# Cross-attention in a decoder layer: one more key tile turned by DMA, fewer PSUM banks for TensorE's turns, two output banks

## The chip, the cores and the metric

The kernel runs on one core of a Trainium2 chip. The metric is device time in microseconds (us) of one execution; a lower time is better.

## The reference

One decoder layer with three parts, each followed by a residual sum and a layer norm. The change touches only the middle one, the cross-attention of 4 x 256 queries to 4 x 1601 keys, with 32 query heads that share 8 key heads of width 128. Cut to what matters:

```python
q = rmsnorm((x @ Wq.T) by heads, q_norm_w)            # 32 heads of 128
k = rmsnorm((ctx @ Wk.T) by heads, k_norm_w)          # 8 heads, each for 4 query heads
v = (ctx @ Wv.T) by heads
scores = einsum('bhqd,bhkd->bhqk', q, k) / sqrt(128) + mask
probs = softmax(scores, axis=-1)
out = einsum('bhqk,bhkd->bhqd', probs, v) @ Wo.T
```

Everything is float32; the kernel reaches that accuracy with two float16 parts of each operand, a high and a low one, and three products of them (high by high, low by high, high by low).

## The kernel before

The attention goes over 32 items (a batch entry and a key head) and cuts each into two units of 512 query rows, 64 units in all. A unit has four query tiles of 128 rows and 13 key tiles of 128 keys (the last holds 65). For each query tile TensorE makes the scores of all 1601 keys in four PSUM banks (`score`, nine matmuls of 416 columns and three of 354: three products in each bank), VectorE takes the mask off and finds the row's extreme (`subtract_mask`), and ScalarE makes the exponentials (`exp`). The probabilities then lie with queries on partitions, and the product with the values needs keys on partitions, so each key tile must be turned.

There are two ways of turning. **By TensorE** (`transpose_p`): four float32 transposes of 128 x 128 into one PSUM bank, then ScalarE casts the bank to the high part (`split_p` in `scalar`) and VectorE subtracts it for the low part (`split_p` in `vector`). The banks for this go round (`t_bank`, `TB` of them), and a turn waits until the low part of `TB` turns ago is made. **By DMA** (`turn_halves`): for each query tile j, an engine first casts the columns of the DMA's key tiles to float16 in `halves` and another subtracts for the low part; GpSimd and VectorE do it for j = 0 and 2, ScalarE and GpSimd for j = 1 and 3. Then the sync engine (SP) issues two transposing DMAs from `halves` into `pT_dma`, one for the high part and one for the low, eight in a unit. Their width is `DW = ND * P`, where `ND` is the number of key tiles that the DMA turns: 7 of 13.

A unit is written as 13 positions, one for each key tile's product with the values (`weigh_values`). Each engine's order is written out by hand: `P_AT` says at which positions the product takes a tile turned by TensorE, `D_AT` where it takes one of the DMA's, `TURN_AT` at which position TensorE turns which tile, `AT` at which positions the scores of the next unit's query tiles are made. All of the product goes into one bank (`o_bank`); VectorE's `take_o` scales it into `o_sb`, and the next unit's product waits for that at position 0.

SP issues every DMA of the attention from one queue, in order: per unit eight transposes (line 2192), four small stores of the inverse sums (line 2199), one load that spreads them to all partitions (`load_inverse`, line 2204, which first waits until those stores have landed), two stores of the output (line 2210), and in every second unit the next keys, queries and their roots (lines 2140 to 2148), in the others the next values (line 2157, and five small ones in line 2163). Each of its waits holds all that stands behind it in the queue. Four units make a trip; the first and the last of 16 trips are written out, and the others are a loop.

Next values are scaled by GpSimd at position 1 of every even unit (`scale_v`, line 2269) and split into their high halves by ScalarE at positions 3 and 6 (`split_v_hi`).

Of the kernel before, what the change touches and what calls it, by code (L numbers as in the profile page):

```python
# [24 lines left out]
P = 128  # L25
# [1917 lines left out]
def attention(chip, mask, qS, kS, vS, rS, iS, oS, output):  # L1943
# [15 lines left out]
    KR = KV - TAIL  # L1959
    HALF = P // 2  # L1960
    assert KR == HALF + 1
    TB = 3
    RING = 4
    BODY = 4
    TRIPS = UNITS // BODY
    ND = 7
    NP = NT - ND
    DW = ND * P
    P_AT = (0, 1, 2, 5, 8, 11)
    P_TILES = (7, 8, 9, 12, 10, 11)  # L1970
    TAIL_AT = P_TILES.index(NT - 1)
    D_AT = [pos for pos in range(NT) if pos not in P_AT]
    AT = {0: 1, 3: 2, 6: 3, 9: 0}
    TURN_AT = {2: 3, 5: 4, 8: 5, 10: 0, 11: 1, 12: 2}
    assert NP * BODY % RING == 0 and NP * BODY % TB == 0 and KP == NT * P and len(P_AT) == NP

    ends = [0, KP, KP + NT * HD, KP + NT * HD + 2 * QW]
# [18 lines left out]
    halves = [chip.at(f"halves{s}", [P, 2 * DW], 44160 + DW * s, F16) for s in range(2)]  # L1996
    pT_dma = [chip.at(f"pT_dma{s}", [P, 2 * ND, QW], place, F16) for s, place in enumerate((46976, 16768))]
    o_sb = chip.at("o_sb", [P, 2, QW], 51456)
    inv_b = chip.at("inv_b", [P, QW], 50560)
    t_min = chip.small("t_min", [P, 2 * QT])  # L2000
    p_sum = chip.small("p_sum", [P, 2 * QT])
    p_inv = chip.small("p_inv", [P, 32])
# [37 lines left out]

    def o_bank(i, u):

        return psum[:, SB - 1 if last_unit(i, u) else SB + TB, :]

    def banked(ap):
        return ap.rearrange("p (b n) -> p b n", b=SB)
# [14 lines left out]
    def last_trip(i):  # L2061
        return isinstance(i, int) and i == TRIPS - 1
# [3 lines left out]

    def last_unit(i, u):
        return last_trip(i) and u == BODY - 1

    def exists(i, u):  # L2070
        return u < BODY or not last_trip(i)
# [63 lines left out]
    def splits_v(i, u):  # L2135
        return not u % 2 and not (last_trip(i) and u)
# [217 lines left out]
    def gpsimd(pool):  # L2354
        def position(i, u, pos):
            after = exists(i, u + 1)
            if pos == 0 and after and not (first_trip(i) and u == 0):
                halves_hi_pool(pool, i, u + 1, 0)
                repeat_tail(pool, i, u + 1, 0)
            if pos == 1 and (splits_kq(i, u) or splits_v(i, u)):  # L2360
                pool.wait_ge(lo_dve, done_down(half_tile(i, u + 1, 0)))
            if pos == 1 and splits_kq(i, u):
                scale(pool, kq_item(i, u)[0])
                split_kq_lo(pool, *kq_item(i, u), 0)
            if pos == 1 and splits_v(i, u):
                scale_v(pool, v_item(i, u)[0])
            if pos == 3 and after:
                halves_lo_pool(pool, i, u + 1, 1)
                repeat_tail(pool, i, u + 1, 1)
            if pos == 5 and after:  # L2370
                halves_hi_pool(pool, i, u + 1, 2)
                repeat_tail(pool, i, u + 1, 2)
            if pos == 6 and splits_kq(i, u):
                split_kq_lo(pool, *kq_item(i, u), 2)
                split_kq_lo(pool, *kq_item(i, u), 1)
            if pos == 6 and splits_v(i, u):
                split_body_lo(pool, *v_item(i, u), 0)
                split_body_lo(pool, *v_item(i, u), 1)
            if pos == 9 and after:
                halves_lo_pool(pool, i, u + 1, 3)  # L2380
                repeat_tail(pool, i, u + 1, 3)
            if pos == 11 and splits_v(i, u):
                split_tail(pool, *v_item(i, u))
            if pos == 11 and first_trip(i):
                rows.root(pool, G // 2 - 1, 1, range(u, u + 1))
            if last_trip(i) and u >= BODY - 3:
                output.early["gpsimd"](pool, u - BODY, pos)

        halves_hi_pool(pool, 0, 1, 0)
        repeat_tail(pool, 0, 1, 0)  # L2390
        for n in range(2):
            split_kq_lo(pool, 1, 1, n)
        schedule(pool, position)
# [44 lines left out]
    def scalar(act):  # L2438
        def split_p(i, u, n):
            m, step = NP * u + n, turn_step(i, u, n)  # L2440
            act.wait_ge(pT_done, done(step))
            act.wait_ge(pv_done, done(pv_before(i, u, n)))
            act.copy(pT_hi[:, m % RING], t_bank(m)).then_inc(pT_hi_act, 1)  # L2443
            if n == TAIL_AT:
                for k, (to, at) in enumerate(((slice(96, 128), slice(32, 64)), (slice(96, 97), slice(64, 65)))):
                    act.wait_ge(pT_hi_act, done(scalar_step(i, u, n) + k))
                    act.copy(pT_lo[to, m % RING], pT_hi[at, m % RING]).then_inc(pT_hi_act, 1)

        def position(i, u, pos):
            after = exists(i, u + 1)  # L2450
            if pos in TURN_AT and exists(i, turn(u, pos)[0]):
                split_p(i, *turn(u, pos))
            if pos in (2, 5, 8) and after:
                exp(act, i, u + 1, TURN_AT[pos] - 2)
            if pos == NT - 1 and exists(i, u + 2):
                exp(act, i, u + 2, 0)
            if pos in (2, 8) and after:
                halves_hi_act(act, i, u + 1, TURN_AT[pos] - 2)
            if pos == 0 and splits_kq(i, u):
                split_kq_hi(act, *kq_item(i, u), 0)  # L2460
                split_kq_hi(act, *kq_item(i, u), 1)
            if pos == 3 and splits_kq(i, u):
                split_kq_hi(act, *kq_item(i, u), 2)
            if pos == 3 and splits_v(i, u):
                split_v_hi(act, *v_item(i, u), 0)
            if pos == 6 and splits_v(i, u):
                split_v_hi(act, *v_item(i, u), 1)
            if last_unit(i, u) and pos == 5:
                for s in range(2):
                    act.wait_ge(turned[s], turn_landed(2 * UNITS - 1))  # L2470
            if last_trip(i) and u >= BODY - 3:
                output.early["scalar"](act, u - BODY, pos)

        for n in range(3):
            split_p(0, 0, n)
        schedule(act, position)
# [100 lines left out]
    def tensor(pe):  # L2577
        def transpose_p(i, u, n):
            m, step, kt = NP * u + n, turn_step(i, u, n), P_TILES[n]
            if n == 0:  # L2580
                pe.wait_ge(e_done, done(tile(i, u, QT - 1)))
            if n == TAIL_AT:
                pe.wait_ge(tail_done, done(tile(i, u, QT - 1)))
            pe.wait_ge(pT_lo_done, done(step - TB))
            for j in range(QT):
                last = pe.transpose(t_bank(m)[:, P * j:P * (j + 1)], p_sb[u % 2][:, j, P * kt:P * (kt + 1)], ident)  # L2586
            last.then_inc(pT_done, 1)

        def weigh_values(i, u, pos):
            slot, kt = u // 2 % 2, tile_of(pos)  # L2590
            d = slice(HD * kt, HD * (kt + 1))
            if pos == 0:
                pe.wait_ge(v_lo_done, done(V_PARTS * (2 * i + u // 2 + 1) - 1))
                if not last_unit(i, u):
                    pe.wait_ge(o_done, done(unit(i, u) - 1))
            if pos == D_AT[0]:
                for s in range(2):
                    pe.wait_ge(turned[s], turn_landed(half_tile(i, u, QT - 1)))
            if kt < ND:
                product(pe, o_bank(i, u), v_hi[slot][:, d], v_lo[slot][:, d], pT_dma[u % 2][:, kt],  # L2600
                        pT_dma[u % 2][:, ND + kt], False, pos == NT - 1).then_inc(pv_done, 1)
                return
            n = P_AT.index(pos)
            m = NP * u + n
            pe.wait_ge(pT_lo_done, done(turn_step(i, u, n)))
            if kt < NT - 1:
                product(pe, o_bank(i, u), v_hi[slot][:, d], v_lo[slot][:, d], pT_hi[:, m % RING], pT_lo[:, m % RING],
                        pos == 0, False).then_inc(pv_done, 1)
                return
            pe.matmul(o_bank(i, u), v_hi[slot][:, d], pT_hi[:, m % RING], start=False, stop=False)  # L2610
            pe.wait_ge(pT_hi_act, done(scalar_step(i, u, n) + 2))
            pe.matmul(o_bank(i, u), v_lo[slot][:, d], pT_lo[:, m % RING], start=False, stop=False).then_inc(pv_done, 1)

        def position(i, u, pos):
            if pos in AT and exists(i, scored(u, pos)[0]):
                score(pe, i, *scored(u, pos))
            weigh_values(i, u, pos)
            if pos in TURN_AT and exists(i, turn(u, pos)[0]):
                transpose_p(i, *turn(u, pos))

        for n in range(3):

            pe.wait_ge(sem("qT_sb_done"), done(TT * G - 1 - 3 + n))
            transpose_p(0, 0, n)
        pe.wait_ge(sem("qT_sb_done"), done(TT * G - 1))
        pe.wait_ge(rows.summed, rows.summed_at(G - 1))
        schedule(pe, position)
# [471 lines left out]
```

## Time and profile before

| | |
|---|---|
| time, median of 3 runs | 2429.32 us (2429.22 to 2430.34) |
| time of the profiled execution | 2432.23 us |
| span from its first to its last instruction | 2430.4 us |
| TensorE (PE) busy | 2383.0 us, 98% |
| VectorE (DVE), ScalarE (ACT), GpSimd (POOL) busy | 75%, 66%, 60% |
| granted TensorE clock, mean | 0.998 of the higher level |
| transposing DMAs | 512, from 951.9 to 2213.3 us of the span |

The span begins with the gated projection and the keys and values, the attention's units begin near 976 us, and the output projection ends the span. Busy time of TensorE is modelled from pipelined matmuls whose times overlap, so a high share doesn't say by itself that TensorE is the limit. SP's issuing of DMAs isn't counted as busy time of an engine on the page; in the trace it appears as SPq, and SPq times are those of the sequencer that issues.

### The profile page before, as it was taken

How to read it: one execution, taken by the hardware profiler on the slowest of the kernel's cores; microseconds unless marked ns; L12 is line 12 of the kernel's file. 1: busy time of each engine (PE TensorE's matmuls, PEld its weight loads, DVE VectorE, ACT ScalarE, POOL GpSimd, SP SyncE). 2: the span in 40 equal slices, each digit the busy share in tenths (PEclk: the TensorE clock that was granted, in tenths of full speed). 3: DMA queues.
4: the chain of work that ended last, by engine and by line, in shares of the span. 5: the costliest groups of instructions: out<-in, count | busy, mean ns of one | idle time of the engine just before them, and what ended most of it. 6: DMA issues, size and time to landing. Idle time of an engine off the chain costs nothing.

```text
span 2430.4 us, 45071 instructions
## 1 busy us (share of the span) xinstructions
PE 2383.0 (98%) x12414; PEld 1650.8 (68%) x12414; DVE 1829.1 (75%) x2707; ACT 1593.3 (66%) x3248; POOL 1463.5 (60%) x1365
## 2 busy tenths in 40 slices
PE   9999999999999999999999999999999999999998
PEld 8878888888888886555555555555555555556887
DVE  5899999996865446777777777777777777776544
ACT  3187787787552556677777777777777777776321
POOL 0077877787640236787777777777777777763000
PEclk9999999999999999999999999999999999999999
DMA  6334433443364446888888888888888888879432
GB/s 232 119 101 120 130 106 110 130 112 112 120 211 135 150 133 199 196 177 194 186 197 182 196 183 202 193 184 197 185 198 183 198 183 200 193 145 244 149 109 65
DMA packets 749053, 398.43 MB, mean 164 GB/s; under 512 B 493265, under 2 KB 696145, under 8 KB 748977
## 3 DMA queue, kind: packets, MB, share of 16 engines
q1 hardware_dynamic: 748976, 397.52, 64.6%
q8 instruction: 35, 0.57, 0.1%
q14 instruction: 42, 0.34, 0.0%
HBM read 183.85 MB, written 96.11 MB: 115 GB/s over the span
## 4 chain that ended last, share of the span: by engine, by line
PE 45%; SPq 33%; issue 10%; DMA 8%; DVE 1%; POOL 1%; ACT 1%; POOLq 0%; ACTq 0%; DVEq 0%
SPq L2192 20%; PE banks L206 12%; PE banks L208 11%; PE banks L207 11%; PE banks L1137 8%; DMA inverse_sums<-p_invT 6%; SPq L2199 3%; SPq L2163 2%; SPq L2210 2%; PE banks L436 2%; SPq L2204 1%; SPq L103 1%; SPq L2140 1%; SPq L2157 1%; SPq L104 1%
## 5 line engine op out<-in xcount | busy, mean ns | idle before, releaser
L1058 DVE TENSOR_SCALAR_CACHE_REDUCE flags<-abs_s,thr 128x1376 bf16<-128x1376 f32 x256 | 403.7, 1643 | 1.1
L2521 DVE TENSOR_TENSOR pT_lo<-banks,pT_hi 128x512 f16<-128x512 f32 (+1 forms) x384 | 257.5, 684 | 157.2 <-ACT pT_hi L2443 157.2
L206 PE MATMUL banks<-k_hi,q_hi 128*128 128x416 f16 (+1 forms) x1024 | 342.9, 335 | 8.9 <-DVE t_min L2482 4.5
L207 PE MATMUL banks<-k_lo,q_hi 128*128 128x416 f16 (+1 forms) x1024 | 341.3, 333 | 0.0
L208 PE MATMUL banks<-k_hi,q_lo 128*128 128x416 f16 (+1 forms) x1024 | 341.1, 333 | 0.0
L2443 ACT CAST pT_hi<-banks 128x512 f16<-128x512 f32 x384 | 215.4, 585 | 161.9 <-PE banks L2586 160.9
L2482 DVE CUSTOM_DVE_ANT_0 p_even<-banks,minus_mask,guard_scalars 128x1664 f32<-128x1664 f32 x128 | 249.2, 1947 | 33.3 <-PE banks L208 33.2
L2482 DVE CUSTOM_DVE_ANT_0 p_odd<-banks,minus_mask,guard_scalars 128x1664 f32<-128x1664 f32 x128 | 249.4, 1948 | 30.3 <-PE banks L208 29.4
L2414 ACT ACTIVATE p_even<-p_even,t_min 128x1601 f32<-128x1601 f32 x128 | 209.3, 1635 | 3.0 <-DVE t_min L2486 2.2
L2414 ACT ACTIVATE p_odd<-p_odd,t_min 128x1601 f32<-128x1601 f32 x128 | 209.2, 1634 | 1.0 <-DVE t_min L2486 0.2
L914 ACT ACTIVATE k_sb<-banks,rstd 128x128 f32<-128x128 f32 x392 | 106.8, 384 | 114.6 <-POOL rstd L810 114.6
L206 PE MATMUL banks<-pT_dma,v_hi 128*128 128x512 f16 x448 | 169.8, 379 | 2.0 <-DMA pT_dma<-halves 2.0
L208 PE MATMUL banks<-pT_dma,v_lo 128*128 128x512 f16 x448 | 169.8, 379 | 0.0
L207 PE MATMUL banks<-pT_dma,v_hi 128*128 128x512 f16 x448 | 169.8, 379 | 0.0
L206 PEld LDWEIGHTS banks<-k_hi,q_hi 128*128 128x128 f16 x1024 | 99.9, 98 | 101.9 <-DVE t_min L2482 31.9
L2309 POOL TENSOR_TENSOR halves<-p_odd,halves 128x896 f16<-128x896 f32 x64 | 120.8, 1888 | 75.5 <-ACT halves L2300 75.5
L206 PE MATMUL banks<-kw_hi,c_hi 128*128 128x512 f32 x400 | 160.4, 401 | 0.6 <-DVE p_sb L350 0.4
L207 PE MATMUL banks<-kw_lo,c_hi 128*128 128x512 f32 x400 | 156.4, 391 | 0.0
L208 PE MATMUL banks<-kw_hi,c_lo 128*128 128x512 f32 x400 | 156.4, 391 | 0.0
L208 PEld LDWEIGHTS banks<-k_hi,q_lo 128*128 128x128 f16 x1024 | 100.4, 98 | 73.7 <-issue 0.4
L207 PEld LDWEIGHTS banks<-k_lo,q_hi 128*128 128x128 f16 x1024 | 100.5, 98 | 61.0 <-issue 0.6
L206 PE MATMUL banks<-pT_hi,v_hi 128*128 128x512 f16 x320 | 121.6, 380 | 18.5 <-DVE o_sb L2536 9.6
(286 smaller groups left out, 6512.3 us busy)
## 6 DMA issues: line engine op xcount, KB each, us to landing
raw<-keys SPq DMA_DIRECT2D x32, 800.5 KB, 4.5
keys<-kT_sb SPq DMA_DIRECT2D x50, 512.0 KB, 5.0
values<-v_sb SPq DMA_DIRECT2D x50, 512.0 KB, 3.6
raw<-values SPq DMA_DIRECT2D x32, 768.0 KB
queries<-qT_sb SPq DMA_DIRECT2D x64, 256.0 KB, 2.7
raw<-queries SPq DMA_DIRECT2D x32, 512.0 KB, 5.3
r_sb<-query_roots SPq DMA_DIRECT2D x32, 512.0 KB, 6.5
inv_b<-inverse_sums SPq DMA_DIRECT2D x64, 256.0 KB, 3.5
```

What stands on the lines that cost most here:

```text
L206: pe.matmul(out, a_hi, b_hi, start=start, stop=False)
L207: pe.matmul(out, a_hi, b_lo, start=False, stop=False)
L208: return pe.matmul(out, a_lo, b_hi, start=False, stop=stop)
L914: last = act.activation(k_sb[:, at], k_banks(s)[:, at], ACT.Copy, scale=rstd[:, s % RING, g:g + 1])
L1058: bits.done(dve.tensor_scalar(flags[:, tt % 2], abs_s[:, tt], thr[:, tt:tt + 1].bitcast(F32), 0.0, ALU.is_lt, ALU.add, accum_out=out[:, tt ...
L1137: last = pe.matmul(out, a[:, k], b, start=start and k + n == 0, stop=k == 1 and n == 2, skip_group_check=not start)
L2192: sp.dma_start_transpose(pT_dma[u % 2][:, ND * part:ND * (part + 1), P * j:P * (j + 1)], halves[j % 2][:, DW * part:DW * (part + 1)]).then ...
L2309: pool.tensor_tensor(halves[1][:, DW:2 * DW], p_sb[u % 2][:, j, 0:DW], halves[1][:, 0:DW], ALU.subtract).then_inc(lo_pool, 1)
L2414: act.activation(at, at, ACT.Exp, bias=t_min[:, n:n + 1], scale=-1.0, accum_out=p_sum[:, n:n + 1]).then_inc(e_done, 1)
L2443: act.copy(pT_hi[:, m % RING], t_bank(m)).then_inc(pT_hi_act, 1)
L2482: dve.tensor_tensor_reduce(banked(p_sb[u % 2][:, j, 0:KP]), psum[:, 0:SB, 0:SW], banked(minus_mask[:, j % 2]), guards.score_scale, 3.40282 ...
L2521: dve.tensor_tensor(pT_lo[r, m % RING], t_bank(m)[r], pT_hi[r, m % RING], ALU.subtract).then_inc(pT_lo_done, 1)
```

## The change

`ND` goes from 7 to 8: the DMA turns key tiles 0 to 7, TensorE tiles 8 to 12, five in place of six. `halves` and `pT_dma` grow with it, and `inv_b` moves to another place. `TB` goes from 3 to 2, and the bank that comes free becomes a second one for the output, so that units take them by turns; the product of a unit waits at position 0 for the output of the unit before the last one, not of the last one. TensorE's turn for the fourth tile stays at position 2, the fifth goes from position 5 to 6, and the sixth is gone. In the first unit alone, GpSimd scales the next values at position 5 and not 1, and ScalarE splits their first half at position 6 and not 3. `EXP_AT` writes out the same order of exponentials as before.

```diff
-    TB = 3
+    TB = 2
...
-    ND = 7
+    ND = 8
...
-    P_AT = (0, 1, 2, 5, 8, 11)
-    P_TILES = (7, 8, 9, 12, 10, 11)
+    P_AT = (0, 1, 2, 5, 9)
+    P_TILES = (8, 9, 10, 12, 11)
...
-    TURN_AT = {2: 3, 5: 4, 8: 5, 10: 0, 11: 1, 12: 2}
+    TURN_AT = {2: 3, 6: 4, 10: 0, 11: 1, 12: 2}
+    EXP_AT = {2: 1, 5: 2, 8: 3}
...
-    inv_b = chip.at("inv_b", [P, QW], 50560)
+    inv_b = chip.at("inv_b", [P, QW], 20864)
...
-        return psum[:, SB - 1 if last_unit(i, u) else SB + TB, :]
+        return psum[:, SB - 1 if last_unit(i, u) else SB + TB + u % 2, :]
...
+    def first_unit(i, u):
+        return first_trip(i) and u == 0
...
-            if pos == 1 and splits_v(i, u):
+            if pos == 1 and splits_v(i, u) and not first_unit(i, u):
                 scale_v(pool, v_item(i, u)[0])
...
+            if pos == 5 and first_unit(i, u):
+                scale_v(pool, v_item(i, u)[0])
...
-            if pos in (2, 5, 8) and after:
-                exp(act, i, u + 1, TURN_AT[pos] - 2)
+            if pos in EXP_AT and after:
+                exp(act, i, u + 1, EXP_AT[pos])
...
-                halves_hi_act(act, i, u + 1, TURN_AT[pos] - 2)
+                halves_hi_act(act, i, u + 1, EXP_AT[pos])
...
-            if pos == 3 and splits_v(i, u):
+            if pos == (6 if first_unit(i, u) else 3) and splits_v(i, u):
                 split_v_hi(act, *v_item(i, u), 0)
...
-                    pe.wait_ge(o_done, done(unit(i, u) - 1))
+                    pe.wait_ge(o_done, done(unit(i, u) - 2))
```

## Rows read from the trace of the kernel before

**Rows 1.** The page's busy times: us, share of the span, instructions.
```profile
PE 2383.0 (98%) x12414; PEld 1650.8 (68%) x12414; DVE 1829.1 (75%) x2707; ACT 1593.3 (66%) x3248; POOL 1463.5 (60%) x1365
```

**Rows 2.** The page's chain that ended last, by engine and by line.
```profile
PE 45%; SPq 33%; issue 10%; DMA 8%; DVE 1%; POOL 1%; ACT 1%; POOLq 0%; ACTq 0%; DVEq 0%
SPq L2192 20%; PE banks L206 12%; PE banks L208 11%; PE banks L207 11%; PE banks L1137 8%; DMA inverse_sums<-p_invT 6%; SPq L2199 3%; SPq L2163 2%; SPq L2210 2%; PE banks L436 2%; SPq L2204 1%; SPq L103 1%; SPq L2140 1%; SPq L2157 1%; SPq L104 1%
```

**Rows 3.** SP's waits, 1060 to 2130 us: us in total, times, longest.
```profile
SPq L104 <- DMA inverse_sums<-p_invT: 30.3, 27, 1.4
```

**Rows 4.** Timeline of SP, part of one pair of units: start, us.
```profile
1661.00 0.39 SPq L2204 DMA_DIRECT2D inv_b<-inverse_sums  x1
...
1677.09 2.58 SPq L2192 DMA_TRANSPOSE pT_dma<-halves  x2
1680.01 0.39 SPq L2204 DMA_DIRECT2D inv_b<-inverse_sums  x1
1680.76 5.37 SPq L2192 DMA_TRANSPOSE pT_dma<-halves  x4
...
1691.44 0.38 SPq L2140 DMA_DIRECT2D raw<-keys  x1
...
1693.35 1.66 SPq L2199 DMA_DIRECT2D inverse_sums<-p_invT  x4
1695.21 3.54 SPq L2192 DMA_TRANSPOSE pT_dma<-halves  x2
1700.51 0.38 SPq L2204 DMA_DIRECT2D inv_b<-inverse_sums  x1
```

**Rows 5.** Pieces of the chain within that pair: start, us, what.
```profile
1674.71 0.23 SPq L2163
...
1694.75 5.46 DMA inverse_sums<-p_invT
```

**Rows 6.** Instructions on `halves`, 1060 to 2130 us: ns min/median/max.
```profile
L2192 SPq DMA_TRANSPOSE pT_dma<-halves x436: 1220/1233/2778, 1059.7 to 2126.4; - x146
L2300 ACT CAST halves<-p_odd x55: 937/938/942, 1062.3 to 2121.6; 128x896 f16<-128x896 f32 x55
L2309 POOL TENSOR_TENSOR halves<-p_odd,halves x55: 1883/1887/1895, 1063.3 to 2122.7; 128x896 f16<-128x896 f32 x55
```

**Rows 7.** Stretches: us, busy of each engine, clock, DMA share, GB/s.
```profile
1060.00:2130.00 1070.00, 1055.71 (x6000) 600.97 (x5999) 835.23 (x1255) 818.93 (x1147) 799.62 (x764) 1.00 0.84 191
...
1682.00:1687.00 5.00, 5.00 (x30) 2.81 (x28) 4.13 (x5) 3.50 (x6) 3.43 (x5) 1.00 1.10 196
1702.00:1707.00 5.00, 4.43 (x26) 2.30 (x25) 4.10 (x5) 4.55 (x7) 4.57 (x8) 1.00 1.00 190
```

**Rows 8.** TensorE's largest waits, 1060 to 2130 us.
```profile
PE banks L206 <- DVE o_sb L2536: 9.6, 17, 1.0
...
PEld banks L206 <- DVE t_min L2482: 26.1, 99, 0.3
PEld banks L206 <- issue: 19.8, 30, 1.4
```

**Rows 9.** Timeline of TensorE, one turn and the matmul behind it.
```profile
1661.78 0.60 PE L2586 MATMUL banks<-ident,p_odd 128*128 128x128 f32 x4
1662.22 0.38 PE L206 MATMUL banks<-pT_dma,v_hi 128*128 128x512 f16 x1
```

**Rows 10.** Three turns in a row: TensorE's third, ScalarE's and VectorE's splits.
```profile
1682.60 0.60 PE L2586 MATMUL banks<-ident,p_even 128*128 128x128 f32 x4
...
1681.38 0.94 ACT L2300 CAST halves<-p_even 128x896 f16<-128x896 f32 x1 [2.04 <-DMA pT_dma<-halves]
1682.23 1.66 ACT L2443 CAST pT_hi<-banks 128x512 f16<-128x512 f32 x3
...
1682.84 1.29 DVE L2521 TENSOR_TENSOR pT_lo<-banks,pT_hi 128x512 f16<-128x512 f32 x2 [1.09 <-ACT pT_hi L2443]
```

**Rows 11.** Waits in the first trip, 978 to 1060 us (GpSimd's 970 to 990).
```profile
POOL raw L2269 <- DMA raw<-values: 6.1, 1, 6.1
...
PE banks L206 <- DVE pT_lo L2521: 3.2, 2, 3.0
...
PEld banks L206 <- DVE pT_lo L2521: 3.9, 2, 3.5
...
SPq L104 <- POOL halves L2294: 3.4, 3, 1.6
SPq L104 <- DMA inverse_sums<-p_invT: 2.8, 2, 1.6
```

## The prediction

> **What bounds the kernel now.** I read the page first. TensorE is busy for 98% of the span, the other engines for 75% and less [rows 1], so a change that takes four transposes from TensorE in each of 64 units looks like a gain at once. The chain that ended last says otherwise: a third of it is SPq, the queue from which SP issues DMAs, and its largest single piece is line 2192, the transposing DMAs of `turn_halves`, with 20% [rows 2]. That is a hint that in the attention the issuing of DMAs sets the pace, and it has to be settled from SP's waits.
>
> I took the stretch from 1060 to 2130 us, which has 436 of the 512 transposes [rows 6], so 436 / 8 = 54.5 units, one in 1070 / 54.5 = 19.63 us. In these 1070 us SP waits for one thing only: 27 times, once in each pair of units, 30.3 us in all, for the landing of its own small stores of the inverse sums [rows 3]. No wait for an engine is listed: whatever GpSimd, ScalarE, VectorE or TensorE had to deliver to SP was there before SP came to it. A queue that waits for nobody and never rests is the pace maker. The timeline shows it from near: between the rows of SP lie a few tenths of a us of register and semaphore work, and the one real hole is between 1698.75 (1695.21 + 3.54) and 1700.51 [rows 4]. It ends with the landing 5.46 us after the last store [rows 5]; those stores stand in the queue behind the next keys and queries [rows 4], which come once in a pair. One transpose of that place also takes longer: two need 3.54 us there and 2.58 elsewhere [rows 4].
>
> TensorE in the same stretch has holes, though small ones: it waits for the lowest score of the tile before (26.1 us), for the output bank (9.6 us) and for things that the profile doesn't name (19.8 us) [rows 8], about 1 us a unit together. They come from SP in a roundabout way: ScalarE stands 2.04 us before its cast for `halves` until a transpose has landed, and the splits of the turned tiles, for which VectorE waits, stand behind that cast [rows 10]. So TensorE is close behind the bound, but it is SP that both wait for.
>
> **The change part by part.**
>
> *SP, eight longer transposes.* One takes 1.233 us of the queue (median of 436, least 1.220) [rows 6]. All move 7 tiles, so no row tells what 8 cost. From below: nothing more, as plain DMAs behave, where the keys' load needs 0.38 us and the far smaller inverse load 0.39 [rows 4]. A fixed part like that 0.38 would leave (1.233 - 0.38) / 7 = 0.122 us for a tile; one like the smallest DMA of the queue, 0.23 [rows 5], 0.143. From above: all of it is by tiles, 1.233 / 7 = 0.176. Less than before is excluded, as no tile gets cheaper by an eighth one beside it. I take 0.176, since a transpose of three times the time of a plain DMA is not a plain DMA's case, and since the DMA engines can't take up a cheaper issue at once: in two stretches where SP issues four transposes one after another their share is 1.10 and 1.00 [rows 7], so they finish a transpose about as slowly as SP issues it (1.33 us from one to the next, 5.37 / 4 [rows 4]), and their packets grow by the seventh for certain.
>
> A page of the Trainium skill speaks against this change at the same point. In "DMA: Bandwidth & Descriptors", section "Why a DMA increments its semaphore by 16 and not by 1", a table on a later chip gives that chip "one DMA push command for the whole transpose instead of one per tile", so that the generations before it pay the issuing sequencer for each tile. By that rule the price is the upper bound, and the sum below is as it stands; by the rows of plain DMAs it would be nothing. No run here shows a second width yet.
>
> So the 436 transposes cost SP 436 x 0.176 = 76.8 us more. A part is hidden: two of each pair's 16 stand between the last store of the inverse sums and its landing, and the wait that ends there has 30.3 / 27 = 1.12 us, more than 2 x 0.176 = 0.35. That takes 27 x 0.35 = 9.5 us off, and 67.3 us stay. That wait would then show 0.77 us each. If the landing moves with the transposes ahead of it, nothing is hidden.
>
> *Casts and differences for `halves`.* They grow by a seventh: ScalarE's from 0.938 to 1.07 us, GpSimd's difference from 1.887 to 2.16 [rows 6]. The path from one transpose's landing over ScalarE's cast and GpSimd's difference to SP's next is 0.17 + 0.13 + 0.27 = 0.57 us longer, while SP itself needs 4 x 0.176 = 0.70 us more between these points; SP waits there for nothing now, and still won't. Cost 0. ScalarE and VectorE each lose one split in a unit; neither bounds, gain 0.
>
> *TensorE's turns.* Four transposes need 0.44 us from one start to the next matmul [rows 9], so TensorE has that much less in each unit, 28.2 us in 64. Where SP sets the pace this becomes idle time of TensorE. The gain is real only where SP has room: in the last four units, when no more keys and values are loaded, 4 x 0.44 = 1.8 us.
>
> *Two turn banks in place of three.* The third turn in a row, at position 12, now waits until the first one's low part is made. Now it starts at 1682.60, while VectorE makes the first two low parts in 1.29 us from 1682.84 [rows 10], the first of them so about 0.65 us later, at 1683.5. This is a new wait of 0.9 us a unit. What stands behind it on TensorE are the scores of the next query tile, then the products at position 0; VectorE's `subtract_mask` and ScalarE's `exp` wait for those scores. It costs nothing while SP gives a unit 19.63 + 67.3 / 54.5 = 20.86 us: TensorE needs 1055.71 / 54.5 = 19.37 us by its modelled busy time [rows 7], 18.93 without the turn, and 19.8 with the wait. Cover left: 1 us.
>
> *Two output banks.* They take away the wait for `take_o`, 9.6 us in the stretch and perhaps part of the 19.8 [rows 8]. TensorE isn't the bound, so 0.
>
> *Next values later in the first unit.* GpSimd stands 6.1 us for the values' landing, with its difference for `halves` behind that, and TensorE waits in this trip for late low parts 3.2 + 3.9 = 7.1 us [rows 11]. In the first trip SP does wait for engines (3.4 us for GpSimd's casts alone, beside 2.8 us for landings [rows 11]), so a gain there is worth something, but SP's 32 transposes of the trip cost 32 x 0.176 = 5.6 us more. Between a gain of 7.1 us and a loss of 5.6 I take a gain of 3. No DMA moves with these edits; the values thus split are first used in the third unit, and the load that writes over their raw copy stands in the second, so the four positions of delay cost nothing there.
>
> Sum: 67.3 - 1.8 - 3 = 62.5 us. The profiled execution took 2432.2 us, 1.8 us more than its span of 2430.4, and would take 2494.7; it stands 2.9 us above the median of the runs shown, 2429.3, so that the forecast for a median is 2429.3 + 62.5 = **2492 us**.
>
> **The rivals.**
>
> *A. The issue doesn't grow* (as with plain DMAs), and SP keeps its 19.63 us a unit. For it: 0.38 and 0.39 us for loads of very different size [rows 4]. Against: the full DMA engines [rows 7]. Then the two small gains are left, 4.8 us: 2424.5 us, on the edge between faster and the same. This is the rival on the other side, and it decides if a transpose of 8 tiles is still issued in 1.23 us.
>
> *B. TensorE is the bound after all*, and the turns come off the end: 28.2 us, and 3 in the first unit: 2398 us. For it: 98% busy. Against: SP without a wait for 1070 us, and a transfer that would have to speed up.
>
> *C. As A, but the wait for the second bank counts:* TensorE needs 19.8 us a unit where SP would give 19.63, 0.2 x 54.5 = 11 us more: 2435 to 2436 us. It needs A first.
>
> *D. The DMA engines become the bound too.* Their share is 0.84 [rows 7], 16.5 us a unit; eight transposes longer by 1.33 / 7 = 0.19 make it 18.0 of the new 20.86, which still fits. But landings that come later, behind the next keys and queries, would add to the forecast: a second wait as long as the 1.12 us of now in every unit is 61 us more, a third of it 20: 2512 to 2550 us.
>
> **How the numbers follow.** Chances: the forecast 0.82, A 0.06, B 0.04, C 0.03, D 0.05. The forecast's own range: at the low end a price of 0.122, 53.2 us, of which 27 x 0.24 = 6.6 are hidden, and 7.1 and 1.8 gained elsewhere, 37.7 us: 2467. At the high end nothing hidden and 5.6 lost in the first trip, 76.8 + 5.6 - 1.8 = 80.6 us: 2510. With almost all of that case and the near part of D, 2465 to 2513 holds 8 in 10. About 0.2% (4.9 us) is what a measurement here can tell from no change. Slower by more: the forecast, C and D, 0.90; faster: B and half of A, 0.07; the same: the other half, 0.03. The likeliest gives the time, 2492.
>
> **What would show it.** Right: the transposes' median near 1.41 us (1.23 under A); SP still without a wait for any engine in the middle of the attention, with the wait for the inverse sums near 0.8 us; units of about 20.9 us; line 2192 with a larger part of the chain; TensorE with new idle time of a us or more a unit, put down to transposes that have not landed or to low parts (the two turn banks), and none for `o_sb`; GpSimd without its 6.1 us in the first unit. Wrong: SP waiting for GpSimd or ScalarE in the middle (the longer casts, or TensorE late by the banks), transposes at 1.23 us, or units at or under 19.6 us.

## The result and the profile after

| | before | after |
|---|---|---|
| median | 2429.83 us (4 runs) | 2469.35 us (2468.03 to 2474.07, 4 runs) |
| profiled execution, span | 2430.4 us | 2467.8 us |

The ratio is 1.0165, with a 95% interval of 1.0148 to 1.0183: 39.5 us slower. The forecast was 62.5 us slower, 2492 us with a range of 2465 to 2513. The direction and the range held; the reason held only in part, as the profile after shows already.

The page after, busy times and the chain that ended last (against [rows 1, 2]):

```profile
span 2467.8 us, 44200 instructions
...
PE 2362.9 (96%) x12158; PEld 1609.6 (65%) x12158; DVE 1813.9 (74%) x2643; ACT 1582.9 (64%) x3184; POOL 1515.0 (61%) x1365
...
PE 53%; issue 11%; SPq 9%; POOL 8%; DVE 8%; DMA 6%; ACT 4%; POOLq 0%; ACTq 0%; DVEq 0%
PE banks L206 15%; PE banks L208 15%; PE banks L207 15%; DMA pT_dma<-halves 4%; SPq L2196 4%; PE banks L2592 3%; PE banks L1137 3%; DVE p_odd L2488 3%; DVE p_even L2488 2%; POOL v_sb L830 2%; SPq L2203 2%; DVE pT_lo L2527 2%; SPq L2167 2%; ACT pT_hi L2449 1%; POOL rstd L810 1%
```

TensorE does 20 us less and the span is 37 us longer. SPq, a third of the chain before, is 9% now, and the chain runs through all engines. That fits a loop, in which each engine waits for the next, better than one queue that never rests.

The transposes, 1060 to 2130 us, with their issue time in ns (least, median, most) and the time to landing (against [rows 6]):

```profile
L2196 SPq DMA_TRANSPOSE pT_dma<-halves x424: 1231/1258/2851, 1061.8 to 2128.4; - x142
...
DMA to landing us min/median/max: 3.0/3.3/5.4
```

A transpose of eight tiles takes 1.258 us to issue in the median, 0.025 more than one of seven, where the forecast had 0.176 more. In this stretch lie 424 / 8 = 53 units, 20.19 us each, where 54.5 lay before. SP's waits in the same stretch (against [rows 3]):

```profile
SPq L104 <- DVE halves L2308: 17.4, 38, 1.3
SPq L104 <- DMA inverse_sums<-p_invT: 17.4, 27, 1.0
SPq L104 <- DVE p_invT L2536: 7.3, 25, 0.3
SPq L104 <- POOL halves L2298: 2.5, 10, 0.3
SPq L2054 <- DMA query_roots<-row_rstd: 1.1, 1, 1.1
```

SP now waits for VectorE and GpSimd, 27 us, so it is not the only pace maker. TensorE's waits, first its matmuls, then its weight loads (the two are views of the same holes and are not added; against [rows 8]):

```profile
PE banks L2592 <- DVE pT_lo L2527: 36.7, 53, 2.8
PE banks L206 <- DVE t_min L2488: 25.5, 53, 0.5
...
PEld banks L206 <- DVE t_min L2488: 68.4, 106, 1.0
PEld banks L2592 <- DVE pT_lo L2527: 62.9, 53, 3.3
PEld banks L206 <- DVE pT_lo L2527: 15.5, 53, 0.4
```

The wait at the turn, line 2592, is new, comes once in every one of the 53 units, and is the wait for one of two turn banks. The chain from one unit to the next shows where it leads (start, us, what):

```profile
1697.46 1.25 SPq L2196
1698.82 3.20 DMA pT_dma<-halves
...
1702.99 0.59 ACT pT_hi L2449
1703.60 0.70 DVE pT_lo L2527
1704.35 0.66 PE banks L2592 x4
...
1711.64 1.95 DVE p_odd L2488
...
1714.27 0.22 DVE p_invT L2536
1714.71 0.30 SPq L2203
...
1716.58 1.25 SPq L2196
```

and TensorE's rows at that turn:

```profile
1703.37 0.38 PE L208 MATMUL banks<-pT_dma,v_lo 128*128 128x512 f16 x1
1704.35 0.66 PE L2592 MATMUL banks<-ident,p_even 128*128 128x128 f32 x4 [0.60 <-DVE pT_lo L2527]
```

The second query tile's transposes land; ScalarE, which stands before its cast for `halves` until then, makes that cast and then the first turn's high part; VectorE makes the low part; only then is TensorE's third turn free to start, at 1704.35; the scores behind it come late, so VectorE's `subtract_mask`, the inverse sums behind that, SP's stores of them, and the next unit's transposes behind those stores. The ring closes in 19.1 us here. The next round, up to 1737.76, takes 21.2 us: its transposes stand behind the next keys and land after 4.16 us, not 3.20, and the way back goes over VectorE's difference for `halves` and SP's issuing of the next values. So it isn't the same chain in every unit.

### The profile page after: what moved, and what is told of

It reads as the page before. It is cut to its first block, busy times and chain, and to the rows that moved or that the text cites. A ratio compares the mean times of both kernels' runs of the same rounds, so it can differ in the third digit from the quotient of the medians.

```text
span 2467.8 us, 44200 instructions
## 1 busy us (share of the span) xinstructions
PE 2362.9 (96%) x12158; PEld 1609.6 (65%) x12158; DVE 1813.9 (74%) x2643; ACT 1582.9 (64%) x3184; POOL 1515.0 (61%) x1365
## 4 chain that ended last, share of the span: by engine, by line
PE 53%; issue 11%; SPq 9%; POOL 8%; DVE 8%; DMA 6%; ACT 4%; POOLq 0%; ACTq 0%; DVEq 0%
PE banks L206 15%; PE banks L208 15%; PE banks L207 15%; DMA pT_dma<-halves 4%; SPq L2196 4%; PE banks L2592 3%; PE banks L1137 3%; DVE p_odd L2488 3%; DVE p_even L2488 2%; POOL v_sb L830 2%; SPq L2203 2%; DVE pT_lo L2527 2%; SPq L2167 2%; ACT pT_hi L2449 1%; POOL rstd L810 1%
## 5 line engine op out<-in xcount | busy, mean ns | idle before, releaser
L2488 DVE CUSTOM_DVE_ANT_0 p_even<-banks,minus_mask,guard_scalars 128x1664 f32<-128x1664 f32 x128 | 249.6, 1950 | 101.4 <-PE banks L208 101.4
L2449 ACT CAST pT_hi<-banks 128x512 f16<-128x512 f32 x320 | 181.4, 585 | 191.8 <-PE banks L2592 187.6
L2527 DVE TENSOR_TENSOR pT_lo<-banks,pT_hi 128x512 f16<-128x512 f32 (+1 forms) x320 | 214.3, 685 | 88.6 <-ACT pT_hi L2449 87.8
L206 PE MATMUL banks<-pT_dma,v_hi 128*128 128x512 f16 x512 | 194.6, 380 | 3.4 <-DMA pT_dma<-halves 3.4
L208 PE MATMUL banks<-pT_dma,v_lo 128*128 128x512 f16 x512 | 194.6, 380 | 0.0
L207 PE MATMUL banks<-pT_dma,v_hi 128*128 128x512 f16 x512 | 194.6, 380 | 0.0
L2313 POOL TENSOR_TENSOR halves<-p_odd,halves 128x1024 f16<-128x1024 f32 x64 | 136.5, 2133 | 77.4 <-ACT halves L2304 77.4
L2313 POOL TENSOR_TENSOR halves<-p_even,halves 128x1024 f16<-128x1024 f32 x64 | 137.1, 2141 | 13.1 <-ACT halves L2304 12.7
```

Source lines behind the costliest of these rows:

```text
L206: pe.matmul(out, a_hi, b_hi, start=start, stop=False)
L207: pe.matmul(out, a_hi, b_lo, start=False, stop=False)
L208: return pe.matmul(out, a_lo, b_hi, start=False, stop=stop)
L2313: pool.tensor_tensor(halves[1][:, DW:2 * DW], p_sb[u % 2][:, j, 0:DW], halves[1][:, 0:DW], ALU.subtract).then_inc(lo_pool, 1)
L2488: dve.tensor_tensor_reduce(banked(p_sb[u % 2][:, j, 0:KP]), psum[:, 0:SB, 0:SW], banked(minus_mask[:, j % 2]), guards.score_scale, 3.40282 ...
L2527: dve.tensor_tensor(pT_lo[r, m % RING], t_bank(m)[r], pT_hi[r, m % RING], ALU.subtract).then_inc(pT_lo_done, 1)
```

## The experiments

In all of them a unit's length is 8 x 1060 us over the number of transposes from 1060 to 2120 us; the kernel before has 434 there, 19.54 us a unit.

**Three turn banks again, one output bank; eight tiles by DMA.**

```diff
-    TB = 2
+    TB = 3
+    BACK = (2, 2, 5, 3, 3)
...
-        return psum[:, SB + m % TB, :]
+        return psum[:, SB + m % NP % TB, :]
...
-        return psum[:, SB - 1 if last_unit(i, u) else SB + TB + u % 2, :]
+        return psum[:, SB - 1 if last_unit(i, u) else SB + TB, :]
...
-            pe.wait_ge(pT_lo_done, done(step - TB))
+            pe.wait_ge(pT_lo_done, done(step - BACK[n]))
...
-                    pe.wait_ge(o_done, done(unit(i, u) - 2))
+                    pe.wait_ge(o_done, done(unit(i, u) - 1))
```

> The changed kernel with three turn banks and one output bank again (a unit's five turns use banks 0, 1, 2, 0, 1); the DMA still turns eight tiles. Theory 1, the turn banks: with two, TensorE's third turn waits for a split that stands on ScalarE behind the landing of a transpose, and a loop over SP closes; with three the wait goes (TensorE's 101 us at line 2592 in the middle stretch fall under 5), SP again waits only for the inverse sums, and a unit takes the old 19.6 us and 8 x 0.025 = 0.2 more: 2434 to 2442 us. Theory 2, the width: the longer casts and landings of eight tiles cost the time, and it stays at 2460 to 2470 us.

2447.26 us, ratio to the kernel before 1.0075 (1.0059 to 1.0092): 22 us of the 39.5 go, 17.4 stay. The edit gives back a turn bank for an output bank, and the wait for `o_sb` is back with it (22.1 us); no run parts the two. Its transposes and SP's waits, 1060 to 2120 us:

```profile
L2197 SPq DMA_TRANSPOSE pT_dma<-halves x427: 1231/1262/2987, 1058.8 to 2119.8; - x143
```

```profile
SPq L104 <- DMA inverse_sums<-p_invT: 18.5, 27, 0.9
SPq L104 <- POOL halves L2314: 0.5, 1, 0.5
```

SP again waits for almost nothing but its own stores, as in the kernel before, so I take it as the pace maker again, at 19.86 us; the single store further down bears this out. Theory 1 holds for the wait at the turn, which is gone, but the time is 5 us above its range: the median transpose is only 0.03 us longer, but those behind the next keys are longer by more. The SP timeline of this kernel, around such loads (against [rows 4]):

```profile
1659.03 1.69 SPq L2204 DMA_DIRECT2D inverse_sums<-p_invT  x4
1660.92 4.06 SPq L2197 DMA_TRANSPOSE pT_dma<-halves  x2
1665.78 0.39 SPq L2209 DMA_DIRECT2D inv_b<-inverse_sums  x1
1666.53 5.52 SPq L2197 DMA_TRANSPOSE pT_dma<-halves  x4
```

Two transposes take 4.06 us there, against 3.54 before: half a us of the 0.64 by which a pair of units grows sits at this one place. The wait that follows falls from 1.12 to 18.5 / 27 = 0.69 us, so a part is hidden there, as the prediction had it.

**The kernel before with two turn banks and two output banks; seven tiles.**

```diff
-    TB = 3
+    TB = 2
...
-        return psum[:, SB - 1 if last_unit(i, u) else SB + TB, :]
+        return psum[:, SB - 1 if last_unit(i, u) else SB + TB + u % 2, :]
...
-                    pe.wait_ge(o_done, done(unit(i, u) - 1))
+                    pe.wait_ge(o_done, done(unit(i, u) - 2))
```

> The kernel before with two turn banks and two output banks, the DMA still at seven tiles. Theory 1, the turn banks: the loop is there with shorter pieces, 0.3 us less of landing and 0.13 us less of a cast than in the changed kernel's 20.0 us a unit, so 19.6 us or slightly more: 2430 to 2440 us, with TensorE waiting 0.5 to 1.5 us a unit at its turns. Theory 2, the width: no loss, 2425 to 2430 us, without such waits.

2439.80 us, ratio 1.0042 (1.0028 to 1.0056): 9.9 us slower, theory 1. SP's waits and the one at the turn:

```profile
SPq L104 <- DMA inverse_sums<-p_invT: 29.7, 27, 1.4
SPq L104 <- DVE p_invT L2530: 11.0, 25, 0.5
SPq L104 <- DVE halves L2304: 9.6, 25, 0.6
```

```profile
PEld banks L2586 <- DVE pT_lo L2521: 38.3, 53, 1.9
```

The same wait as in the changed kernel, with shorter pieces around it. The exchange of banks alone costs 9.9 us, the width alone (with the positions and the first unit's edit, which came along) 17.4; together they cost 39.5, which is 12 more than the sum. That fits a ring on which the longer landing and cast lie once two banks close it; no run parts these pieces.

**ScalarE's cast behind the first turn's split; two banks, eight tiles.**

```diff
-            if pos in (2, 8) and after:
-                halves_hi_act(act, i, u + 1, EXP_AT[pos])
+            if pos in (2, 10) and after:
+                halves_hi_act(act, i, u + 1, 1 if pos == 2 else 3)
```

> The changed kernel, but ScalarE's cast for the fourth query tile's transposes stands at position 10 behind the first turn's split, not at position 8 ahead of it. Theory 1, the turn banks: the splits no longer wait for a landing, the loop is cut with both turn banks kept, and the time falls to 2434 to 2450 us (the fourth tile's transposes come about 1 us later, which may cost a part). Theory 2, the width: no gain, 2465 us or more.

2458.12 us, 11.2 less than the changed kernel. The unit falls from 20.19 to 19.95 us (425 transposes), and the wait at the turn from 61.6 us in the same stretch to

```profile
PEld banks L2592 <- DVE pT_lo L2527: 12.7, 54, 0.2
```

So the wait at the turn does come through this cast: one instruction later in ScalarE's order and most of it is gone. The time lies between the two theories, 8 us above the range of the first and 7 below that of the second: the cut gives half of what the third bank gives. TensorE then waits for low parts at line 206 instead (38.9 us in the weight loads' view, 15.2 in the changed kernel).

**The kernel before with one output store for two.**

```diff
-            for j in range(S // P):
-                sp.dma_start(oS[BODY // 2 * i + u // 2, j, :, heads].rearrange("d (h q) -> d h q", h=2),
-                             o_sb[:, u % 2].rearrange("d (h q) -> d h q", h=2)[:, :, j * P:(j + 1) * P]
-                             ).then_inc(o_out[u % 2], 16)
+            sp.dma_start(oS[BODY // 2 * i + u // 2, :, QW * (u % 2):QW * (u % 2 + 1)], o_sb[:, u % 2]
+                         ).then_inc(o_out[u % 2], 16)
...
+        sp.dma_start(o_raw[:, n % OR].rearrange("p (h q) -> p h q", h=4),
+                     oS[t // 2 * QUADS + c].rearrange("d (h s) -> d h s", h=4)[:, :, t % 2 * P:(t % 2 + 1) * P]
```

> The kernel before, but each unit's output goes out in one DMA and not two (the attended tensor lies otherwise in memory, and the output projection reads it in pieces of 512 bytes). If SP's issuing sets the pace of the kernel before: 0.97 less about 0.41, 0.56 us less in each of 54 units, 30 us, as far as TensorE lets it: 2399 to 2412 us. If TensorE sets it: 2428 to 2431 us.

2416.57 us, ratio 0.9952 (0.9935 to 0.9968): 13.3 us faster with one DMA less a unit in SP's queue. The output projection reads its input otherwise too, but the gain lies in the attention: its first transpose starts 1246.1 us before its last, 1261.4 in the kernel before. SP did set the pace of the kernel before. But only 13 of the expected 30 us come, and the time is 5 us above the range. SP's waits say why:

```profile
SPq L104 <- DMA inverse_sums<-p_invT: 28.2, 28, 1.4
SPq L104 <- DVE halves L2301: 18.0, 40, 0.6
SPq L104 <- DVE p_invT L2527: 12.5, 27, 0.5
SPq L104 <- POOL halves L2291: 4.6, 15, 0.5
SPq L104 <- POOL halves L2306: 2.5, 12, 0.3
```

Now it waits 37.6 us for engines. A second limit of 19.36 us a unit (438 transposes) stood about 0.2 us behind the first. It is close to the 19.37 us that the prediction read as TensorE's modelled work, and TensorE's waits are down to little more than the one for the lowest score (25.6 us in the weight loads' view), so TensorE is the likely second limit; no run tests that.

**Eight tiles, three banks, one output store** (the first and the fourth edit together).

> Eight tiles by DMA, three turn banks, one output bank, and the output stored in one DMA; the transposes as in the changed kernel. If SP set the pace of the kernel with three turn banks (19.8 us a unit): 0.56 us a unit less at most, as long as no loop stands in the way as it did at 19.3 us in the kernel before: 2415 to 2430 us. If the width of eight tiles itself sets it: 2445 us, no gain.

2421.19 us (2418.85 to 2425.11), ratio 0.9963 (0.9948 to 0.9978): 26 us less than without the single store, and 438 transposes again, 19.36 us. Here 0.50 of the 0.56 us a unit come, so SP did set the pace with three banks and eight tiles. With SP relieved, eight tiles are 4.6 us from seven. That doesn't tell how much of the width's 17.4 us was SP's time, since the kernel of seven tiles met its second limit first. Eight tiles leave TensorE 0.44 us less to do in a unit [rows 9]; this is the likely reason that the relief pays almost in full where seven tiles got less than half.

**The high and the low part in one transpose**, of 14 tiles in the kernel before, and of 16 with eight tiles, three banks and the single store.

```diff
-        return landed(TT // 2 + 2 * n + 1)
+        return landed(TT // 2 + n)
...
-        for part, ready in enumerate(((hi_pool, hi_act), (lo_dve, lo_pool))):
-            wait_apart(sp, ready[j % 2], done_down(n), sp_passed)
-            sp.dma_start_transpose(pT_dma[u % 2][:, ND * part:ND * (part + 1), P * j:P * (j + 1)],
-                                   halves[j % 2][:, DW * part:DW * (part + 1)]).then_inc(turned[j % 2], 16)
+        wait_apart(sp, (lo_dve, lo_pool)[j % 2], done_down(n), sp_passed)
+        sp.dma_start_transpose(pT_dma[u % 2][:, :, P * j:P * (j + 1)], halves[j % 2][:]).then_inc(turned[j % 2], 16)
```

> The kernel before with the two transposes of a query tile (high and low part, seven tiles each) issued as one of 14 tiles, once the low part is ready: four in a unit, not eight. It tells what a transpose's issue costs. If the price is by tiles (0.176 us each): 14 x 0.176 = 2.5 us each, SP has as much to issue as before, and the time stays at 2425 to 2435 us. If it is nearly fixed (0.03 us a tile, as 7 against 8 tiles showed): 1.4 to 1.5 us each, 4 us a unit less for SP, which then waits for engines; the unit goes to the next loop, 19.3 us as with the single output store, or longer by the later start of the high parts: 2405 to 2430 us.

> Eight tiles by DMA, three turn banks, one output bank, the output stored in one DMA and one transpose of 16 tiles for each query tile. If the issue price is nearly fixed: SP has 14 to 15 us of work a unit and no longer bounds; TensorE's 18.5 us or a loop over a landing sets the unit, 18.6 to 19.6 us: 2375 to 2435 us. If the price is by tiles: SP needs 19.3 us and waits for nobody, 2410 to 2420 us, with transposes of 2.8 us.

2424.24 us (ratio 0.9975, 0.9965 to 0.9986) and 2446.84 us (1.0064, 1.0046 to 1.0082). The first lies in the range for a nearly fixed price; the second is slower than either of its two ranges. The transposes of the first and of the second kernel:

```profile
L2191 SPq DMA_TRANSPOSE pT_dma<-halves x217: 1295/1532/3972, 1064.0 to 2118.4; - x109
DMA to landing us min/median/max: 3.9/4.1/6.6
```

```profile
L2196 SPq DMA_TRANSPOSE pT_dma<-halves x215: 1315/1913/4302, 1061.0 to 2119.7; - x108
DMA to landing us min/median/max: 4.2/4.4/7.5
```

The least issue time is 1.220, 1.231, 1.295 and 1.315 us for 7, 8, 14 and 16 tiles: (1.315 - 1.220) / 9 = 0.011 us a tile on a fixed 1.15. That is the least, and few of the wide transposes reach it. The medians rise faster (1.233, 1.258, 1.532, 1.913), and the means over the same stretch faster still: 1.30 in the kernel before, 1.34 in the changed one and 1.36 with three banks, 1.79 and 2.33 here. So one tile more costs 0.01 to 0.05 us, far from 0.176, but the price isn't fixed: from 7 to 16 tiles the mean grows by 0.11 us a tile. The landing grows too: 3.0, 3.3, 4.1 and 4.4 us. SP has room then (105.8 us of waits for GpSimd's `halves` alone in the first of these kernels), yet little is gained there, 6.7 us, and the second kernel is 25.7 us slower than the same with two transposes. Each high part now waits for its low part and each transpose lands later; which of the two costs more isn't shown.

**The first unit's edit undone in the changed kernel** (values scaled at position 1 and split from position 3).

> The changed kernel with the values of the first unit scaled and split where the kernel before does it (positions 1 and 3). If the edit saves what the prediction took: 3 us slower than the changed kernel, 2471 to 2474 us, with GpSimd's 6 us wait back. If the first trip is held by something else: 2468 to 2470 us.

2472.58 us (2468.44 to 2475.09), 3.2 more than the changed kernel's 2469.35 (2468.03 to 2474.07). The runs overlap, so the gain of 3 us isn't shown. Nor does the first trip show one: from the first transpose to the 33rd the profiled executions take 89.2 us with the edit and 88.0 without. GpSimd's longest wait in this kernel's first unit is still before the scaling of the values, 4.9 us, now put down to VectorE's `halves`; in the changed kernel it is 7.6 us for ScalarE's. The wait moved to another place.

**Inverse sums made and stored earlier**, ahead of the next keys and values in SP's queue, in three kernels: the one before with the single store, the one of eight tiles with three banks and the single store, and the changed kernel.

```diff
-            if pos == 3:
+            if pos == 1:
                 invert(i, u)
...
             if pos == 2 and after:
                 turn_halves(sp, i, u + 1, 0)
+            if pos == 2:
+                store_inverse(i, u)
...
-            if pos == 4:
-                store_inverse(i, u)
```

> The kernel before with the output stored in one DMA and the inverse sums made at position 1 and stored at position 2, ahead of the next keys and values in SP's queue, not at 3 and 4 behind them. If the landing behind the keys is a real part of SP's pace: the 28 us of waits for the inverse sums go, VectorE's p_invT no longer holds SP, and the unit falls from 19.34 us to 19.0 to 19.2, TensorE's 18.9 being the floor: 2397 to 2410 us. If the landing only fills time that another loop sets: 2414 to 2419 us, as with the single store.

> Eight tiles, three turn banks, one output bank, one output store, and the inverse sums early as in the run beside it. If SP and the loop over the inverse sums still set its pace at 19.32 us a unit: 18.8 to 19.1 us, 2390 to 2410 us, at or below the kernel beside it with seven tiles. If the width of eight tiles sets a loop of its own (ScalarE's cast behind a landing): 2415 to 2422 us, no gain.

> The changed kernel, two turn banks and two output banks, with the inverse sums early. The chain of the changed kernel closes its loop from the third turn over the scores, VectorE's inverse sums and SP's stores to the next transpose. If that is the edge that binds: SP no longer waits for p_invT, the loop loses about 2 us of it and falls to SP's own pace or the next edge, 2440 to 2460 us. If it is only the last of several edges: 2463 to 2470 us.

2461.71, 2479.57 and 2556.70 us: slower by 45.1, 58.4 and 87.4 us than the same kernels without the edit. All three expectations failed. The waits for the stores did go, but the second tile's transposes now stand right behind the next keys, queries and roots, where the four stores had stood between. SP's timeline in the last of the three:

```profile
1677.44 0.40 SPq L2144 DMA_DIRECT2D raw<-keys  x1
1678.02 0.37 SPq L2151 DMA_DIRECT2D raw<-queries  x1
1678.65 0.39 SPq L2152 DMA_DIRECT2D r_sb<-query_roots  x1
1679.25 6.27 SPq L2196 DMA_TRANSPOSE pT_dma<-halves  x2
1685.95 0.34 SPq L2208 DMA_DIRECT2D inv_b<-inverse_sums  x1
```

Two transposes take 6.27 us to issue, against 3.93 in the changed kernel, and the latest landing is 7.5 us, against 5.4. In the first of the three, TensorE then waits once in each pair of units for a low part (2.3 us in all without the edit):

```profile
PEld banks L206 <- DVE pT_lo L2518: 44.8, 26, 4.5
```

That is as much as the 45.1 us lost. In the second this wait grows from 17.9 to 73.0 us, most of its 58.4; in the changed kernel the one at the turn grows from 61.6 to 101.4, less than half of its 87.4. So a later landing of this one pair of transposes is dear, and dearer with two turn banks than with three. Whether the inverse sums are an edge of the ring of their own isn't shown, as the landing moved with them.

**The next keys and values loaded at position 7** in the kernel with the single output store.

```diff
-            if pos == 3 and not last_trip(i):
+            if pos == 7 and not last_trip(i):
```

> The kernel before with the output stored in one DMA and the next keys and values loaded at position 7, behind the second tile's transposes and the load of the inverse sums, not at position 3 ahead of them. If the landing of the second tile's transposes behind these loads is what holds the units (it went up with the inverse sums moved, and the time with it): those transposes land in about 3 us in every unit, SP loses its wait for the inverse sums, and a unit falls from 19.34 us to 19.0 to 19.2: 2397 to 2412 us. If the third and fourth tiles' transposes, now behind the loads, hold TensorE at position 3 instead: 2417 to 2440 us.

2482.89 us, ratio 1.0221 (1.0199 to 1.0244), 66 us above the single store alone. Now the third and fourth tile's transposes stand behind the loads, and TensorE meets their landing at position 3:

```profile
PE banks L206 <- DMA pT_dma<-halves: 52.2, 31, 3.8
```

```profile
L2192 SPq DMA_TRANSPOSE pT_dma<-halves x414: 1220/1232/3726, 1063.7 to 2119.9; - x138
DMA to landing us min/median/max: 2.9/3.0/8.7
```

This is the second half of that expectation, and dearer than it said.

The fastest kernel here is the one before with the single output store, 2416.57 us.

## Why the prediction was right, and where not

*SP sets the pace of the kernel before.* Right: relieving its queue by one DMA a unit gave 13.3 us, though TensorE was 98% busy. The next limit lies 0.2 us a unit behind; the prediction had seen TensorE close, with 19.37 us of 19.63.

*The price of a transpose, 0.176 us for the eighth tile.* Wrong, and the largest term of the sum. From seven tiles to eight it is 0.011 us by the least issue time, 0.025 to 0.03 by the median and about 0.05 by the mean. The prediction took the upper bound because plain DMAs are three times cheaper and because the DMA engines were full in two stretches. The first says nothing on growth. The second may stand behind the longer landings at eight tiles and the longer issues at 14 and 16, but no run tests it. For one tile more the rows of plain DMAs (0.38 and 0.39 us for loads of very different size) were the better guide. The Trainium skill's table ("DMA: Bandwidth & Descriptors", section "Why a DMA increments its semaphore by 16 and not by 1") gives the generations before the later chip one push for each tile; the step from there to a price that is all by tiles was the prediction's. That step isn't borne out by these transposes: from 7 to 16 tiles the least issue time rises by 8%, where all by tiles would more than double it. A push for each tile beside a fixed part isn't excluded by them.

*The sum for SP, 67.3 us.* Mis-sized: with three banks, where SP sets the pace, the width costs 17.4 us, and the single store gets it back. An estimate from the means comes near: 436 x 0.053 = 23 us of longer issue, of which 27 x 0.43 = 12 are hidden in the shorter wait for the stores (0.35 a pair forecast); what the other 6 us are isn't shown. The largest single piece of the longer issue sits in the two transposes behind the next keys (3.54 to 4.06 us), which the prediction had counted as hidden, and most of it is.

*The two turn banks, cost 0 with 1 us of cover.* Wrong, and the larger part of the loss: in exchange for the second output bank they cost 22.1 us at eight tiles, 9.9 at seven. The step named the wait, its place and what stands behind it, and sized it at 0.9 us a unit; the turn that the chain shows starts at 1704.35, where the matmul ahead of it, 0.22 us before the next free place, would have let it start at 1703.59, so 0.8 us is about its size. The mistake was to set it against TensorE's own work in a unit. A wait isn't only time on one engine: this one ties TensorE to a landing that SP issues, while SP waits through the scores and VectorE for TensorE. The cover was wrong as well: it was SP's forecast 20.86 us a unit, and SP with eight tiles needs 19.86. Rival C, which said that this wait counts where the issue doesn't grow, came nearest, with 11 us for it; but it too counted the wait as TensorE's time and not as part of a ring.

*Casts, cost 0.* Measured as forecast (1.045 us for 1.07, 2.132 for 2.16). With three banks SP waits 0.5 us for them in the whole stretch, so they cost little there; with two they lie on the ring, and are likely part of the 12 us by which the two edits cost more together.

*Two output banks, 0.* The wait for `o_sb` (9.6 us) went as forecast; the output bank was never tried without the lost turn bank, so its own worth isn't shown.

*TensorE's 28.2 us less.* As forecast it became idle time: the page has 20 us less of modelled busy time, and the span is longer.

*The first unit, a gain of 3.* Not shown either way. GpSimd's 6.1 us did go, and another wait of 7.6 us stands in their place. The 7.1 us that were to be had add two views of the same holes, TensorE's matmuls and its weight loads, so there was about half of that.

By its own signs the prediction fails in part: the transposes' median (1.258 us, not 1.41) was to show rival A, and SP, which was to wait for no engine in the middle, waits 27 us for VectorE and GpSimd; TensorE's new wait of over a us a unit for low parts came as it said.

So the direction is only half earned: an SP that sets the pace does lose by wider transposes, but the larger part of the loss came from a term put at nothing. That the time fell into the range, near its low end, is luck, from two errors that partly cancelled: 45 us too much for the width with the small gains at both ends (62.5 against 17.4), 22 too little for the banks.

## What to carry to other kernels

A queue without waits can be the pace maker, even beside an engine at 98%; relieve it to find out. But ask how far the next limit is, since two limits a percent apart make one-sided gains small. A wait for a freed buffer is to be followed around until it comes back to its own start: if the ring it closes goes through a transfer's landing, its price isn't the wait but the ring's length against the unit's. Ask of a small transfer between a large load and an urgent one what will stand behind the load once it is moved: here the move cost 45 to 87 us, more than the wait that it removed.

## What the runs showed of the hardware

A transposing DMA's least issue time hardly grows with its width: 1.220 us for 7 tiles of 128 x 128, 1.315 for 16. The mean grows more, from 1.30 to 2.33 us, and the landing from 3.0 to 4.4 us in the median. Behind the next keys, queries and roots in the same queue the issue of two transposes grows, from 2.6 us to 3.5 (seven tiles, four small stores between) or 5.7 (none between), and with eight tiles to 3.9 or 6.3. Behind the next values it stays at 2.6.
